# Two elementwise passes of a graph network: moving one operand of each VectorE operation from SBUF to PSUM

## The chip, the cores and the metric

The kernel runs on one core of a Trainium2 chip. The metric is the device time of one execution in microseconds (us). Engine names are those of the profile: PE (TensorE), DVE (VectorE), ACT (ScalarE), POOL (GpSimd), SP (SyncE, which here only issues transfers).

## The reference

Two graph layers on 6250 nodes of 512 features and 100000 edges, each with a layer norm and a ReLU ahead of it and a residual behind it. The change lies in the end of the second layer:

```python
score = exp(clip(einsum('ehd,ehd->eh', K[src], Q[dst]) * scale, -5, 5))   # 8 heads of 64
wV = segment_sum(V[src] * score, dst)
Z  = segment_sum(score, dst)
h  = h1 + wV / (Z + 1e-6)          # h1: the layer's input after norm and ReLU
mean, var = h.mean(0), h.var(0)    # over the 6250 nodes
out = x1 + (h - mean) * rsqrt(var + 1e-5) * gamma + beta
```

The last line is computed as `out = A*h + (x1 + C)`, with A and C one row of 512 numbers each, which stand repeated on all 128 partitions.

## The kernel before

The nodes lie in 49 windows of 128 (the last has 106). `sums` is a tile of SBUF that holds, for each window, 512 columns of wV and 8 columns of Z. Stages run one after the other, each a block that all engines leave together: preparation and layer 0, `dense` (norm, transposes and the three products of layer 1), `attend` (the gather over edges, which fills `sums`), and the three that matter here.

**First pass, `attended`.** DVE adds 1e-6 to all Z at once (L1280), takes their reciprocals in place (L1282), and then does two operations for each window: `weight` (L1288), which multiplies the window by its inverse counts, and `add_h1` (L1293), which adds the window of h1, both in place in `sums`. DVE's order is written out: weight of window w+1, then add_h1 of window w. SP loads h1 from HBM into four buffers in turn (L1234, 256 KB each); the load of window w waits for add_h1 of window w-4 (semaphore `made`, which starts at 4). Behind add_h1, three engines form the sums over the nodes: PE adds up the columns of the window with a matmul against ones (L926), ACT squares the window into one of four buffers `sq` (L1267), and POOL adds that square to `S2` (L1248, two inputs in SBUF) and waits for its own result before the next. None of these three holds DVE back, but the block ends only when all are done.

**Coefficients.** A and C are made from the sums in a chain of short operations (L967 to L1007).

**Last pass, `finish`.** SP loads x1 into four buffers in turn (L1317); the load of window w waits for the result of window w-4 (`done`, which starts at 4). POOL adds C to x1 in place (`shift`, L1341, two inputs in SBUF). DVE does two operations for each window: `scale` (L1353, window times A, in place) and `add` (L1360, window plus x1 into one of four buffers `o`). Its order is scale of window w+1, then add of window w. The add of window w waits for POOL's shift, for the scale, and for the store of window w-4, which has used the same `o`. ACT issues the stores (L1328) as soon as an add is done.

Of the kernel before, what the change touches and what calls it, by code (L numbers as in the profile page):

```python
# [24 lines left out]
ds = bass.ds  # L25
# [6 lines left out]
def build(nc, x, src, dst, W_l, b_l, W_r, gamma0, beta0, Wq, Wk, Wv, gamma1, beta1, out):  # L32
# [44 lines left out]
    with life:  # L77
# [1141 lines left out]
        def attended(S1, S2):  # L1219
            with ExitStack() as ctx:  # L1220
                h1 = sb(ctx, "h1b", [P, NB, D])
                sq = sb(ctx, "sq1", [P, NB, D])
                ps_1 = pb(ctx, "ps_1", [P, 512])
                zero2, h_in, inverse, weighted, made, squared, summed1, summed2 = (
                    sem("zeroed_S2"), sems("h_in2", NB), sem("inverse"), sem("weighted"), sem("h_made2"), sem("squared1"),
                    sem("summed1b"), sem("summed2b"))

                @nc_block()
                def _(block):
                    @block.sync  # L1230
                    def _(sp):
                        def load(w, b):
                            sp.wait_ge(made, w + 1)
                            sp.dma_start(h1[:, b, :], h1_d[ds(w * P, P), :]).then_inc(h_in[b], 16)  # L1234

                        with sp.Fori(0, FOURS) as i:
                            for b in range(NB):
                                load(NB * i + b, b)
                        load(WINDOWS - 1, 0)

                    @block.gpsimd
                    def _(pool):
                        nc.gpsimd.memset(S2[:, :], 0.0).then_inc(zero2, 1)
                        pool.wait_ge(zero2, 1)

                        def add_square(w, b, n=P):
                            pool.wait_ge(squared, w + 1)
                            nc.gpsimd.tensor_tensor(S2[0:n, :], S2[0:n, :], sq[0:n, b, :], ALU.add).then_inc(summed2, 1)  # L1248
                            pool.wait_ge(summed2, w + 1)

                        with pool.Fori(0, FOURS) as i:
                            for b in range(NB):
                                add_square(NB * i + b, b)
                        add_square(WINDOWS - 1, 0, LAST)

                    @block.tensor
                    def _(pe):
                        column_sums(pe, ps_1, made, NB, summed1)

                    @block.scalar  # L1260
                    def _(act):
                        def square(w, b):
                            act.wait_ge(made, w + NB + 1)
                            if not isinstance(w, int) or w >= NB:
                                act.wait_ge(summed2, w - NB + 1)
                            alone(act)
                            nc.scalar.activation(sq[:, b, :], window(w), ACT.Square).then_inc(squared, 1)  # L1267

                        for w in range(NB):
                            square(w, w)  # L1270
                        with act.Fori(1, FOURS) as i:
                            for b in range(NB):
                                square(NB * i + b, b)
                        square(WINDOWS - 1, 0)

                    @block.vector
                    def _(dve):
                        dve.sem_inc(made, NB)
                        weights = sums[:, :].rearrange("p (w c) -> p w c", c=WIDTH)[:, :, D:WIDTH]
                        nc.vector.tensor_scalar(weights, weights, 1e-6, None, ALU.add).then_inc(inverse, 1)  # L1280
                        dve.wait_ge(inverse, 1)
                        nc.vector.reciprocal(weights, weights).then_inc(inverse, 1)  # L1282
                        dve.wait_ge(inverse, 2)

                        def weight(w):
                            v = window(w).rearrange("p (h d) -> p h d", h=HEADS)
                            z = sums[:, ds(w * WIDTH + D, HEADS)].unsqueeze(2).to_broadcast([P, HEADS, DH])
                            nc.vector.tensor_tensor(v, v, z, ALU.mult).then_inc(weighted, 1)  # L1288

                        def add_h1(w, i, b):  # L1290
                            dve.wait_ge(h_in[b], 16 * (i + 1))
                            dve.wait_ge(weighted, w + 1)
                            nc.vector.tensor_tensor(window(w), window(w), h1[:, b, :], ALU.add).then_inc(made, 1)  # L1293

                        weight(0)
                        with dve.Fori(0, FOURS) as i:
                            for b in range(NB):
                                weight(NB * i + b + 1)
                                add_h1(NB * i + b, i, b)
                        add_h1(WINDOWS - 1, FOURS, 0)  # L1300
                        dve.wait_ge(summed1, WINDOWS)
                        share_of(S1, ps_1)


        def finish(A_bc, C_bc):
            with ExitStack() as ctx:
                x1 = sb(ctx, "x1b", [P, NB, D])
                o = sb(ctx, "o", [P, NB, D])
                x_in, shifted, scaled, done, stored = sems("x_in3", NB), sem("shifted"), sem("scaled1"), sem("done"), sems("stored_", NB)

                @nc_block()
                def _(block):
                    @block.sync
                    def _(sp):
                        def load(w, b):
                            sp.wait_ge(done, w + 1)
                            sp.dma_start(x1[:, b, :], x1_d[ds(w * P, P), :]).then_inc(x_in[b], 16)  # L1317

                        with sp.Fori(0, FOURS) as i:
                            for b in range(NB):  # L1320
                                load(NB * i + b, b)
                        load(WINDOWS - 1, 0)

                    @block.scalar
                    def _(act):
                        def store(w, b, n=P):
                            act.wait_ge(done, w + NB + 1)
                            act.dma_start(out[ds(w * P, n), :], o[0:n, b, :]).then_inc(stored[b], 16)  # L1328

                        with act.Fori(0, FOURS) as i:  # L1330
                            for b in range(NB):
                                store(NB * i + b, b)
                        store(WINDOWS - 1, 0, LAST)
                        for b in range(NB):
                            act.wait_ge(stored[b], 16 * (FOURS + (b == 0)))

                    @block.gpsimd
                    def _(pool):
                        def shift(w, i, b):
                            pool.wait_ge(x_in[b], 16 * (i + 1))  # L1340
                            nc.gpsimd.tensor_tensor(x1[:, b, :], x1[:, b, :], C_bc[:, :], ALU.add).then_inc(shifted, 1)  # L1341

                        with pool.Fori(0, FOURS) as i:
                            for b in range(NB):
                                shift(NB * i + b, i, b)
                        shift(WINDOWS - 1, FOURS, 0)

                    @block.vector
                    def _(dve):
                        dve.sem_inc(done, NB)  # L1350

                        def scale(w):
                            nc.vector.tensor_tensor(window(w), window(w), A_bc[:, :], ALU.mult).then_inc(scaled, 1)  # L1353

                        def add(w, i, b):
                            dve.wait_ge(shifted, w + 1)
                            dve.wait_ge(scaled, w + 1)
                            if not isinstance(i, int) or i:
                                dve.wait_ge(stored[b], 16 * i)  # L1359
                            nc.vector.tensor_tensor(o[:, b, :], window(w), x1[:, b, :], ALU.add).then_inc(done, 1)  # L1360

                        scale(0)
                        for w in range(NB):
                            scale(w + 1)
                            add(w, 0, w)
                        with dve.Fori(1, FOURS) as i:  # L1366
                            for b in range(NB):
                                scale(NB * i + b + 1)
                                add(NB * i + b, i, b)
                        add(WINDOWS - 1, FOURS, 0)  # L1370

# [36 lines left out]
```

## Time and profile before

| | us |
|---|---|
| median of 3 runs (3610.95 to 3612.53) | 3612.53 |
| the profiled execution | 3613.78 |
| its span, from the first instruction to the last | 3611.8 |
| first pass: DVE's first operation of the block to POOL's last | 3365.0 to 3480.3 |
| coefficients | 3480.8 to 3490.8 |
| last pass: first scale to last add | 3491.4 to 3604.6 |

Times of instructions are counted from the span's start. An engine's busy time is the time in which one of its instructions is under way, whether it moves data or is held up after its start; so a long instruction of a known size is the thing to look at, not the busy share. Two instructions of DVE overlap a little: the next starts before the one ahead of it has ended.

### The profile page before, as it was taken

How to read it: one execution, taken by the hardware profiler on the slowest of the kernel's cores; microseconds unless marked ns; L12 is line 12 of the kernel's file. 1: busy time of each engine (PE TensorE's matmuls, PEld its weight loads, DVE VectorE, ACT ScalarE, POOL GpSimd, SP SyncE). 2: the span in 40 equal slices, each digit the busy share in tenths (PEclk: the TensorE clock that was granted, in tenths of full speed). 3: DMA queues.
4: the chain of work that ended last, by engine and by line, in shares of the span. 5: the costliest groups of instructions: out<-in, count | busy, mean ns of one | idle time of the engine just before them, and what ended most of it. 6: DMA issues, size and time to landing. Idle time of an engine off the chain costs nothing. (4 is left out here: it accounts for less than half of the span.)

```text
span 3611.8 us, 59603 instructions
## 1 busy us (share of the span) xinstructions
PE 2939.7 (81%) x11648; PEld 1500.4 (42%) x11649; DVE 2479.0 (69%) x4591; ACT 1625.9 (45%) x6212; POOL 1891.1 (52%) x1929
## 2 busy tenths in 40 slices
PE   4977767777677774999989999999999999999640
PEld 2432222222222222888864444444444444444210
DVE  4643333333333334555559999999999999999999
ACT  2530000000000001222239999999999999999410
POOL 1017777777777771111135555555555555555456
PEclk9997787777777776999999999999999999999865
DMA  2447777777777772444459898888989889888347
GB/s 87 146 144 207 207 208 207 208 207 206 208 207 208 208 207 90 151 152 148 145 213 314 310 313 310 311 309 311 311 308 311 307 311 311 312 308 313 97 123 214
DMA packets 263475, 828.03 MB, mean 229 GB/s; under 512 B 35237, under 2 KB 35239, under 8 KB 263402
## 3 DMA queue, kind: packets, MB, share of 16 engines
q0 software_dynamic: 197504, 693.22, 59.4%
q1 hardware_dynamic: 58910, 121.60, 10.4%
q10 hardware_dynamic: 7020, 12.80, 0.9%
q14 instruction: 32, 0.26, 0.0%
q8 instruction: 9, 0.15, 0.0%
HBM read 750.45 MB, written 77.83 MB: 229 GB/s over the span
## 5 line engine op out<-in xcount | busy, mean ns | idle before, releaser
L1064 POOL DMA_INDIRECT kv<-kv_d,src_t x880 | 828.2, 941 | 677.4 <-PE psw L1204 510.4
L822 POOL DMA_INDIRECT rows<-y_d,src_t x880 | 844.1, 959 | 486.7 <-issue 244.6
L1085 ACT ACTIVATE kv<-kv,wgt 128x64 f32<-128x64 f32 x4400 | 1096.9, 334 | 0.0
L1201 PE MATMUL psa<-kv,hot 128*128 128x512 f32 x1760 | 863.4, 613 | 29.2 <-ACT kv L1085 28.0
L909 PE MATMUL pss<-rows,hot 128*128 128x512 f16 x1760 | 556.9, 447 | 276.0 <-DMA rows<-y_d,src_t 252.5
L1110 DVE TENSOR_TENSOR kv<-kv,ps_q 128x1024 f32<-128x1024 f32 x440 | 534.6, 1215 | 35.8 <-PE ps_q L1185 20.7
L1123 DVE TENSOR_REDUCE score<-kv 128x16 f32<-128x1024 f32 x440 | 533.5, 1212 | 0.0
L1007 ACT ACTIVATE var<-var 128x512 f32<-128x512 f32 x2 | 1.3, 629 | 1134.9 <-DVE var L994 1134.9
L1201 PEld LDWEIGHTS psa<-kv,hot 128*128 128x128 f32 x1760 | 303.6, 189 | 396.1 <-issue 386.9
L1185 PE MATMUL ps_q<-sums,hotT 128*128 x1760 | 454.9, 381 | 0.0
L843 DVE TENSOR_SCALAR rd<-psc 128x1 f32 (+1 forms) x49 | 7.8, 159 | 547.0 <-PE psc L911 547.0
L909 PEld LDWEIGHTS pss<-rows,hot 128*128 128x128 f16 x1760 | 120.0, 104 | 470.5 <-issue 411.4
L1204 PE MATMUL psw<-parts,hot 128*128 128x16 f32 x880 | 302.0, 415 | 0.0
L836 DVE TENSOR_TENSOR hot<-lane,rel_t 128x256 f16<-128x256 f32 x440 | 187.3, 426 | 163.3 <-issue 98.4
L344 POOL TENSOR_TENSOR x_sb<-x_sb,C_bc 128x512 f32<-128x512 f32 x49 | 63.5, 1297 | 410.7 <-DMA x_sb<-in_x 410.7
L1204 PEld LDWEIGHTS psw<-parts,hot 128*128 128x128 f32 x880 | 167.5, 190 | 211.0 <-issue 211.0
L1116 DVE TENSOR_TENSOR kv<-kv,wgt 128x384 f32<-128x384 f32 x440 | 242.6, 551 | 0.3 <-ACT wgt L1078 0.3
L510 PE MATMUL ps_o<-w_hi,hT_hi 128*128 128x512 f32 x588 | 239.5, 407 | 0.0
L510 PE MATMUL ps_o<-w_hi,hT_lo 128*128 128x512 f32 x588 | 232.2, 395 | 0.0
L510 PE MATMUL ps_o<-w_lo,hT_hi 128*128 128x512 f32 x588 | 231.7, 394 | 0.0
L1185 PEld LDWEIGHTS ps_q<-sums,hotT 128*128 128x128 f16 x1760 | 172.8, 98 | 110.6 <-issue 2.6
L893 PE MATMUL psz<-w_r,sums 128*128 128x512 f16 x588 | 214.7, 541 | 0.0
(185 smaller groups left out, 3550.8 us busy)
## 6 DMA issues: line engine op xcount, KB each, us to landing
kv_d<-o_sb SPq DMA_DIRECT2D x49, 512.0 KB, 2.9
rows<-y_d,src_t POOLq DMA_INDIRECT x880, 3.7
kv<-kv_d,src_t POOLq DMA_INDIRECT x880, 5.3
y_d<-y SPq DMA_DIRECT2D x49, 256.0 KB, 2.0
x_d<-x_sb SPq DMA_DIRECT2D x49, 256.0 KB, 3.2
h_d<-h SPq DMA_DIRECT2D x49, 256.0 KB, 3.4
h1b<-h_d SPq DMA_DIRECT2D x49, 256.0 KB, 2.7
x1b<-x_d SPq DMA_DIRECT2D x49, 256.0 KB, 4.0
```

The costliest lines, as they stand in the source:

```text
L510: last = nc.tensor.matmul(ps_o[par][k][:, :], a, b[:, k, c, :], start=(c == 0 and j == 0), stop=(c == KC - 1 and j == 2))
L822: pool.indirect_dma_start(rows[:, u, g, :], None, y_d[0:N, :], bass.IndirectOffsetOnAxis(src_t[:, m:m + 1], 0)).then_inc(rows_in[u], 16)
L893: nc.tensor.matmul(psz[:, ds(par, D)], slots[:, ds(at * 2 + part * D + c * P, P)], w_r16[:, of, c, :], start=(c == 0 and part == of == 0), ...
L909: nc.tensor.matmul(pss[:, ds(par, D)], hot[:, u, g, :], rows[:, u, g, part * D:(part + 1) * D], start=False, stop=(g == G - 1 and part == ...
L1064: pool.indirect_dma_start(kv[:, u, g, :], None, kv_d[0:N, :], bass.IndirectOffsetOnAxis(src_t[:, m:m + 1], 0)).then_inc(rows_in[u], 16)
L1085: last = nc.scalar.mul(v, v, wgt[:, u, g * HEADS + h:g * HEADS + h + 1])
L1110: nc.vector.tensor_tensor(k, k, ps_q[u % 2][:, :].rearrange("p (g d) -> p g d", g=G), ALU.mult).then_inc(multiplied, 1)
L1116: nc.vector.tensor_tensor(v, v, w.unsqueeze(3).to_broadcast([P, G, HEADS - HA, DH]), ALU.mult)
L1123: nc.vector.tensor_reduce(score[:, u, :].rearrange("p (g h) -> p g h", g=G), kv[:, u, :, 0:D].rearrange("p g (h d) -> p g h d", h=HEADS), ...
L1185: last = nc.tensor.matmul(ps_q[u % 2][:, g * D:(g + 1) * D], hotT[:, u % 2, g * P:(g + 1) * P], slots[:, ds(col * 2 + k * D, D)], start=(k ...
L1201: nc.tensor.matmul(pss[:, ds(par, D)], hot[:, u, g, :].bitcast(F32), kv[:, u, g, D:2 * D], start=False, stop=(g == G - 1), skip_group_chec ...
L1204: last = nc.tensor.matmul(psc[:, 0:2 * HEADS], hot[:, u, g, :], parts[:, u % 4, g, :, :].rearrange("p t h -> p (t h)"), start=False, stop= ...
```

## The change

The two passes keep their operations, their number and their order. Each operation of DVE now takes one of its two inputs from PSUM:

- the reciprocals are written to a tile `z_inv` in PSUM instead of back into `sums`;
- `weight` reads the window from SBUF and the inverse counts from PSUM, and writes to one of four tiles `ps_v` in PSUM;
- `add_h1` reads `ps_v` and h1 (SBUF), and writes the window in `sums`;
- A is copied once to `A_ps` in PSUM;
- `scale` reads the window from SBUF and A from PSUM, and writes to one of four tiles `ps_a` in PSUM;
- `add` reads `ps_a` and x1 (SBUF), and writes `o`.

As the four PSUM tiles are used in turn, `weight` and `scale` get a wait on the result of four windows earlier.

```diff
@@ attended
+                z = pb(ctx, "z_inv", [P, WINDOWS * HEADS])
+                ps_v = [pb(ctx, f"ps_v{k}", [P, D]) for k in range(NB)]
-                        nc.vector.reciprocal(weights, weights).then_inc(inverse, 1)
+                        nc.vector.reciprocal(z[:, :].rearrange("p (w h) -> p w h", h=HEADS), weights).then_inc(inverse, 1)
-                        def weight(w):
+                        def weight(w, b):
+                            dve.wait_ge(made, w + 1)
                             v = window(w).rearrange("p (h d) -> p h d", h=HEADS)
-                            z = sums[:, ds(w * WIDTH + D, HEADS)].unsqueeze(2).to_broadcast([P, HEADS, DH])
-                            nc.vector.tensor_tensor(v, v, z, ALU.mult).then_inc(weighted, 1)
+                            nc.vector.tensor_tensor(ps_v[b][:, :].rearrange("p (h d) -> p h d", h=HEADS), v,
+                                                    z[:, ds(w * HEADS, HEADS)].unsqueeze(2).to_broadcast([P, HEADS, DH]),
+                                                    ALU.mult).then_inc(weighted, 1)
@@ add_h1
-                            nc.vector.tensor_tensor(window(w), window(w), h1[:, b, :], ALU.add).then_inc(made, 1)
+                            nc.vector.tensor_tensor(window(w), ps_v[b][:, :], h1[:, b, :], ALU.add).then_inc(made, 1)
@@ finish
+                A_ps = pb(ctx, "A_ps", [P, D])
+                ps_a = [pb(ctx, f"ps_a{k}", [P, D]) for k in range(NB)]
+                A_in = sem("A_in")
+                        nc.vector.tensor_copy(A_ps[:, :], A_bc[:, :]).then_inc(A_in, 1)
+                        dve.wait_ge(A_in, 1)
-                        def scale(w):
-                            nc.vector.tensor_tensor(window(w), window(w), A_bc[:, :], ALU.mult).then_inc(scaled, 1)
+                        def scale(w, b):
+                            dve.wait_ge(done, w + 1)
+                            nc.vector.tensor_tensor(ps_a[b][:, :], window(w), A_ps[:, :], ALU.mult).then_inc(scaled, 1)
@@ add
-                            nc.vector.tensor_tensor(o[:, b, :], window(w), x1[:, b, :], ALU.add).then_inc(done, 1)
+                            nc.vector.tensor_tensor(o[:, b, :], ps_a[b][:, :], x1[:, b, :], ALU.add).then_inc(done, 1)
```

The calls of `weight` and `scale` get the number of the buffer, `(b + 1) % NB`, as their second argument.

## Rows read from the trace of the kernel before

**Rows 1.** The page: busy tenths of DVE, and GB/s, in 40 equal slices.
```profile
DVE  4643333333333334555559999999999999999999
...
GB/s 87 146 144 207 207 208 207 208 207 206 208 207 208 208 207 90 151 152 148 145 213 314 310 313 310 311 309 311 311 308 311 307 311 311 312 308 313 97 123 214
```

**Rows 2.** Busy time of each engine in the two passes, granted clock, DMA share, GB/s.
```profile
3371.00:3479.00 108.00, 72.27 (x98) 20.27 (x96) 106.71 (x94) 30.25 (x48) 68.90 (x48) 0.75 0.39 109
3495.00:3603.00 108.00, 0.00 (x0) 0.00 (x0) 106.46 (x95) 0.00 (x0) 73.11 (x49) 0.50 0.78 225
```

**Rows 3.** Instruction groups, 3280 to 3612 us: busy us, mean ns | idle before.
```profile
L1353 DVE TENSOR_TENSOR sums<-sums,A_bc 128x512 f32 (+1 forms) x49 | 62.0, 1267 | 0.6 <-PEq L102 0.6
...
L1293 DVE TENSOR_TENSOR sums<-sums,h1b 128x512 f32 (+1 forms) x49 | 58.8, 1202 | 0.0
L1288 DVE TENSOR_TENSOR sums<-sums (+1 forms) x49 | 57.9, 1183 | 0.0
L1360 DVE TENSOR_TENSOR o<-sums,x1b 128x512 f32<-128x512 f32 x49 | 54.5, 1114 | 3.8 <-POOL x1b L1341 3.8
```

**Rows 4.** Timeline of the first pass, two windows: start us, duration us, engine, line.
```profile
3421.22 1.35 POOL L1248 TENSOR_TENSOR S<-S,sq 128x512 f32<-128x512 f32 x1 [1.53 <-ACT sq L1267]
3421.37 1.75 DVE L1288 TENSOR_TENSOR sums<-sums  x1
...
3422.73 1.51 POOL L1248 TENSOR_TENSOR S<-S,sq 128x512 f32<-128x512 f32 x1 [0.16 <-POOL S L1248]
3423.05 1.75 DVE L1293 TENSOR_TENSOR sums<-sums,h1b 128x512 f32 x1
3424.72 0.68 DVE L1288 TENSOR_TENSOR sums<-sums  x1
```

**Rows 5.** Timeline of POOL in the first pass: its first and last operation.
```profile
3371.04 1.50 POOL L1248 TENSOR_TENSOR S<-S,sq 128x512 f32<-128x512 f32 x1 [5.62 <-ACT sq L1267]
...
3479.06 1.26 POOL L1248 TENSOR_TENSOR S<-S,sq 106x512 f32<-106x512 f32 x1 [0.23 <-POOL S L1248]
```

**Rows 6.** Timeline of the last pass: its start and its end.
```profile
3491.42 1.29 DVE L1353 TENSOR_TENSOR sums<-sums,A_bc 128x512 f32<-128x512 f32 x2 [0.62 <-PEq L102]
...
3495.39 0.69 DVE L1360 TENSOR_TENSOR o<-sums,x1b 128x512 f32<-128x512 f32 x1 [2.68 <-POOL x1b L1341]
...
3602.28 2.35 DVE L1360 TENSOR_TENSOR o<-sums,x1b 128x512 f32<-128x512 f32 x2
```

**Rows 7.** Timeline of the dense stage: two places where POOL and DVE meet.
```profile
1416.84 1.42 POOL L344 TENSOR_TENSOR x_sb<-x_sb,C_bc 128x512 f32<-128x512 f32 x1 [21.26 <-DMA x_sb<-in_x]
1417.16 1.64 DVE L384 TENSOR_TENSOR x_sb<-x_sb 128x512 f32<-128x512 f32 x1
...
1832.73 1.29 POOL L344 TENSOR_TENSOR x_sb<-x_sb,C_bc 128x512 f32<-128x512 f32 x1 [11.85 <-DMA x_sb<-in_x]
...
1833.17 0.69 DVE L355 TENSOR_TENSOR hT_lo<-ps_t,hT_hi 128x512 fp32r<-128x512 f32 x1
```

**Rows 8.** Line L407, a copy from PSUM in the dense stage: ns min/median/max.
```profile
L407 DVE COPY o_sb<-ps_o x49: 691/692/693, 1431.1 to 1854.7; 128x512 f32<-128x512 f32 x49
```

**Rows 9.** Tile x1b, POOL's shift in the last pass: ns min/median/max.
```profile
L1341 POOL TENSOR_TENSOR x1b<-x1b,C_bc x49: 1256/1521/1813, 3494.1 to 3602.1; 128x512 f32<-128x512 f32 x49
```

**Rows 10.** Timeline of PE in the first pass: two windows are four matmuls.
```profile
3411.29 3.57 PE L926 MATMUL ps<-sums,ones 128*128 x4 [1.28 <-DVE sums L1293]
3415.84 2.33 PE L926 MATMUL ps<-sums,ones 128*128 x4 [0.97 <-DVE sums L1293]
```

**Rows 11.** DMA issues of the two passes: KB each, median us to landing.
```profile
h1b<-h_d SPq DMA_DIRECT2D x44, 256.0 KB, 2.7
...
result<-o ACTq DMA_DIRECT2D x47, 256.0 KB, 4.2
x1b<-x_d SPq DMA_DIRECT2D x45, 256.0 KB, 4.0
```

**Rows 12.** Waits of SP's queue in the last pass: us in total, times, longest.
```profile
SPq L1317 <- DVE o L1360: 75.2, 45, 2.9
```

More of the change, by code:

```diff
@@ L1292, in add_h1 @@
                             dve.wait_ge(weighted, w + 1)
-                            nc.vector.tensor_tensor(window(w), window(w), h1[:, b, :], ALU.add).then_inc(made, 1)
-                        weight(0)
+                            nc.vector.tensor_tensor(window(w), ps_v[b][:, :], h1[:, b, :], ALU.add).then_inc(made, 1)
+                        weight(0, 0)
                         with dve.Fori(0, FOURS) as i:
                             for b in range(NB):
-                                weight(NB * i + b + 1)
+                                weight(NB * i + b + 1, (b + 1) % NB)
                                 add_h1(NB * i + b, i, b)
@@ L1359, in add @@
                                 dve.wait_ge(stored[b], 16 * i)
-                            nc.vector.tensor_tensor(o[:, b, :], window(w), x1[:, b, :], ALU.add).then_inc(done, 1)
-                        scale(0)
+                            nc.vector.tensor_tensor(o[:, b, :], ps_a[b][:, :], x1[:, b, :], ALU.add).then_inc(done, 1)
+                        scale(0, 0)
                         for w in range(NB):
-                            scale(w + 1)
+                            scale(w + 1, (w + 1) % NB)
                             add(w, 0, w)
@@ L1367, in _ @@
                             for b in range(NB):
-                                scale(NB * i + b + 1)
+                                scale(NB * i + b + 1, (b + 1) % NB)
                                 add(NB * i + b, i, b)
```

## The prediction

> **What bounds the kernel now.** I read the page's slices first, to see which stretch the change can touch. DVE is busy nine tenths or more from the middle of the kernel to its end, and the rate of the transfers drops sharply in the slices ahead of the last [rows 1]: the two changed passes are the last three slices or so, about 225 us of 3612. What comes before them is not edited and I leave it alone.
>
> Next the two passes by themselves, as stretches [rows 2]: DVE is busy for 106.7 of 108 us in the one and 106.5 of 108 in the other. That looks like DVE as the bound, so the next view is what its instructions take, by line [rows 3]. All four kinds are 128 x 512 fp32, one element per lane and step, yet their means lie between 1114 and 1267 ns. A mean over equal shapes that is that uneven in four lines asks for the single instructions, and the timeline gives them [rows 4]: an operation takes either 0.68 or 1.75 us. The reader is to look at what POOL does beside each long one. POOL begins a tensor_tensor with two SBUF inputs at 3421.22; DVE's operation begins at 3421.37 and takes 1.75. The next POOL operation begins at 3422.73, DVE's at 3423.05, and that takes 1.75 again; then comes one of 0.68 with no POOL operation just begun. Successive DVE operations overlap by 0.08 (3423.05 + 1.75 = 3424.80, and the next starts at 3424.72), so a free one costs 0.60 and a held one 1.67. The difference, 1.07 us, is the hold. One window has two DVE operations and one POOL operation: 2 x 0.60 + 1.07 = 2.27 us. Over 48 windows that is 109 us, which is what both passes take: the first from POOL's start at 3371.04 to 3480.32 [rows 5], the last from the first add at 3495.39 to that of the last window, 0.68 before the merged row's end at 3604.63 [rows 6]. So DVE is "busy", but for 1.07 of each 2.27 us it stands behind POOL.
>
> Does PSUM free it? The dense stage shows both cases [rows 7]. At 1417.16 a DVE addition with both inputs in SBUF (L384) begins 0.32 us into a POOL addition and takes 1.64. At 1833.17 one with an input in PSUM and one in SBUF (L355) begins 0.44 us into a POOL addition, ends before it, and takes 0.69. A copy out of PSUM (L407), which in that stage usually meets POOL's addition, never takes more than 693 ns in 49 [rows 8]. So POOL holds DVE where both of DVE's inputs are in SBUF, and not where one is in PSUM. That is the case of all four changed operations.
>
> **The first pass, part by part.** Nothing is removed but the holds: 48 x 1.07 = 51 us of DVE. DVE would then need 2 x 0.60 = 1.20 us a window. What is late next? POOL. Its own operation without DVE in the way is the last one of the pass, 1.26 us, on 106 partitions but as many columns [rows 5]; the shortest of 49 in the last pass, on 128, is 1.256 [rows 9]. Between two of them it waits 0.16 us for its own result [rows 4], so 1.42 us a window. From the same start, 3371.04, it ends at 48 x 1.42 + 1.26 = 69.4 us later, 3440.5, where it now ends at 3480.3. **Gain 39.9 us.** ACT's squares need 30.25 / 48 = 0.63 a window [rows 2] and follow. PE's two matmuls need 2.33 / 2 = 1.17 where they are short [rows 10], below 1.42. h1 lands 2.7 us after its issue [rows 11]; with the add behind it, 0.7, and some 0.3 of handing over, a buffer's lap is 3.7 us, and DVE comes back to a buffer after 4 x 1.20 = 4.8. This cover goes only if the landing grows above 3.8; until POOL itself starved it would have to reach 4.7.
>
> The reciprocal into PSUM stays one instruction. The new wait of weight (window w behind add_h1 of w-4) is met 4.8 us before it is asked; behind it stands only the following add_h1. I price both at nothing; if the wait were ever open, DVE has 0.22 us a window to give before POOL notices.
>
> **The last pass.** The copy of A and its wait come ahead of the first scale: about 0.7 us, one operation of this size, plus a handover. Now DVE does two scales from 3491.42 to 3492.71 and then idles 2.68 us for the first shift [rows 6], which covers the copy; without cover it would cost 0.8. The scale's new wait is met three adds earlier. From the first add on, the holds go (1.07 a window), and again something else is late. POOL's shift allows 1.26. The ring of buffers allows less: an add lets SP load the next window into the buffer, 4.0 us to land [rows 11], 1.26 for the shift, 0.68 for the add, and some 0.3 for three handovers: 6.2 us for a lap of four windows, 1.56 a window. Now the lap is 4 x 2.27 = 9.1, so it has slack, and SP's queue stands waiting for DVE's add, 45 times and 1.67 us each [rows 12]; these loads and the stores (4.2 us to land, no shift behind them, so a lap of 5.2) will start sooner. What they collide with is each other: load and store of one window are released by the same add, 512 KB in all, and the DMA engines are already taken for 0.78 of the time at 225 GB/s [rows 2]. At full share and the same time per packet that is 288 GB/s, or 524288 B / 288 = 1.82 us a window. The fastest long stretches of the page reach 307 to 314 GB/s [rows 1], which would be 1.67. I take 1.70 (308 GB/s), as the stretch of the page is sustained and the 288 is scaled from packets that also queue; the ends are 1.56 (lap at today's landing) and 1.82. **Gain 48 x (2.27 - 1.70) = 27.4 us**, between 21.6 and 34.1.
>
> A page rates such transfers higher: the Trainium skill, "SBUF — State Buffer", section "Summary: rules for kernel authors", has about 358 GB/s for transfers between HBM and SBUF. By it 512 KB would be 1.46 us, an estimate from that page, and the transfers would not be the bound; no run here shows that rate with 2 KB rows going both ways.
>
> **Sum.** 3613.78 - 39.9 - 27.4 = 3546.5 by the profiled execution, which lies 1.25 above the median of the runs. The median would be 3545; I add 0.8 for the copy, should its cover fail: **3546 us**, 1.8% faster.
>
> **Rivals.**
> *PE ends the first pass.* The same two windows take PE 3.57 us instead of 2.33 in places [rows 10], and the granted clock of the pass is 0.75 of full [rows 2], so it changes between its two levels, 2.4 and 1.2 GHz. At 3.57 / 2 = 1.79 a window throughout, the pass would last 49 x 1.79 = 88 us, a gain of 21 instead of 40: 3564. Against it: PE idles 1 to 2 us between its groups now, and will be fed a window each 1.2 us, hence have work always.
> *The transfers are no bound in the last pass.* If landings fall toward the 2.7 us that loads without stores show [rows 11], the lap is 4.9 / 4 = 1.23 and POOL's 1.26 decides: up to 48 x (1.70 - 1.26) = 21 us more, 3525 to 3540. Against: the share of 0.78.
> *Operations that write PSUM are dear.* No DVE operation of the trace writes PSUM. Reading it costs 0.69 against 0.68. If a write doubled the 0.60 of weight and scale, DVE would need 1.80 a window in both passes: 2 x 48 x 0.47 = 45 us of gain, 3568. The Trainium skill ("Perfetto Trace Analysis", "Optimizing Scalar/DVE Operations") puts a DVE access to PSUM at about 125 ns against 60 for SBUF; an estimate by that page is a pair of 1.33 us, which would use up most of DVE's margin to POOL but not the gain. The reads of the trace show 10 to 15 ns.
> *The hold stays.* If POOL held DVE for one SBUF input too, or if DVE held by its PSUM output, both passes keep 2.27: 3613, no change. Against it stands L355.
> *Slower.* The same price of a PSUM write decides. weight or scale would have to cost more than 0.60 + 1.07 = 1.67 us, 2.8 times the read, for the pair to pass 2.27; at three times, 1.80 + 0.60 = 2.40 a window, 2 x 48 x 0.13 = 12 us lost, 3625. Nothing in the rows points there.
>
> **Numbers.** Chances: forecast 0.66 (its own range 3537 to 3554); PE 0.08; no transfer bound 0.10; dear writes 0.08; hold stays 0.04; slower 0.04. The range from 3534 to 3564 takes in the forecast, PE and half of the faster case, 0.79. Faster by more than 0.2% (7 us, about what a measurement of this kernel can tell from no change): 0.92; same 0.04; slower 0.04.
>
> **What would show it.** First pass: no DVE operation above 0.75 us; POOL's squares at 1.26 each and back to back at 1.42, DVE done some 10 us before POOL, a pass of about 70 us. If PE decides, L938 waits for PE long after POOL's end. Last pass: DVE idle before the adds, waiting for POOL's shift, and POOL waiting for x1; a DMA share near 0.95 at about 308 GB/s; landings of 4.3 to 5 us. Long DVE operations that begin inside a POOL operation would refute the release; uniform ones above 0.75 us would mean a dear PSUM access.

## The result, and the profile after

The changed kernel takes 3547.3 us (median of 4 runs, 3544.1 to 3547.9) against 3612.5: a ratio of 0.982, 95% interval 0.980 to 0.984. The forecast was 3546. The profiled execution took 3547.64 us; its span is 3545.7.

Where the 66.1 us between the two profiled executions lie, from the start and end times of the two traces:

| stretch | before | after | difference |
|---|---|---|---|
| up to POOL's first square (edited only in its last 6 us) | 3371.0 | 3369.3 | -1.8 |
| POOL's first square to the end of its last | 109.3 | 72.5 | -36.8 |
| on to DVE's first operation of the last pass | 11.1 | 12.4 | +1.3 |
| on to the first add | 4.0 | 5.1 | +1.1 |
| first add to the end of the last add | 109.2 | 79.5 | -29.7 |
| the last store | 7.2 | 7.0 | -0.2 |

The groups by line of the changed kernel, 3280 to 3546 us (busy us, mean ns of one, idle time of the engine before them and what ended it), answer to [rows 3]:

```profile
L1250 POOL TENSOR_TENSOR S<-S,sq 128x512 f32<-128x512 f32 (+1 forms) x49 | 62.2, 1270 | 15.9 <-POOL S L1250 10.1 <-ACT sq L1269 5.8
L1348 POOL TENSOR_TENSOR x1b<-x1b,C_bc 128x512 f32<-128x512 f32 x49 | 61.6, 1263 | 34.7 <-DMA x1b<-x_d 34.1
...
L1371 DVE TENSOR_TENSOR o<-ps_a,x1b 128x512 f32<-128x512 f32 x49 | 33.9, 691 | 21.1 <-POOL x1b L1348 20.8
L1364 DVE TENSOR_TENSOR ps_a<-sums,A_ps 128x512 f32<-128x512 f32 x49 | 33.5, 686 | 0.0
L1290 DVE TENSOR_TENSOR ps_v<-sums,z_inv 128x512 f32 (+1 forms) x49 | 33.4, 684 | 0.0
L1297 DVE TENSOR_TENSOR sums<-ps_v,h1b 128x512 f32 (+1 forms) x49 | 33.0, 676 | 0.0
```

Every DVE operation is back at 0.67 to 0.70 us: the means have fallen from between 1114 and 1267 ns and are now even, which is the sign that nothing holds them. The two traces bear this out operation by operation. Before, 96 of the 196 DVE operations of the two passes begin while a POOL addition is under way, and 94 of these take 1.73 us or more; of the other 100 none takes more than 0.70. After, 124 begin while a POOL addition is under way, and none takes more than 0.70. POOL's operations gain as well, 1.27 against 1.43 to 1.52, since DVE no longer stands in their way either. The idle time has changed hands: DVE, which had almost none, now waits 20.8 us for POOL's shift.

The two passes as stretches, the first and then the last, answer to [rows 2]:

```profile
3371.00:3441.00 70.00, 52.56 (x96) 14.29 (x94) 54.94 (x92) 29.60 (x47) 59.90 (x48) 0.91 0.56 165
...
3460.00:3538.00 78.00, 0.00 (x0) 0.00 (x0) 60.02 (x94) 0.00 (x0) 59.46 (x48) 0.50 0.93 309
```

The timeline of the first pass (PE's, then POOL's and DVE's rows) answers to [rows 4, 5, 10]:

```profile
3368.51 58.27 PE L926 MATMUL ps<-sums,ones 128*128 128x512 f32 x98 [6.44 <-DVE sums L1297]
...
3369.29 1.27 POOL L1250 TENSOR_TENSOR S<-S,sq 128x512 f32<-128x512 f32 x1 [5.62 <-ACT sq L1269]
...
3373.58 1.27 POOL L1250 TENSOR_TENSOR S<-S,sq 128x512 f32<-128x512 f32 x1 [0.16 <-POOL S L1250]
3373.75 0.68 DVE L1297 TENSOR_TENSOR sums<-ps_v,h1b 128x512 f32 x1
3374.35 0.69 DVE L1290 TENSOR_TENSOR ps_v<-sums,z_inv 128x512 f32 x1
...
3375.26 1.27 POOL L1250 TENSOR_TENSOR S<-S,sq 128x512 f32<-128x512 f32 x1 [0.41 <-POOL S L1250]
...
3440.54 1.26 POOL L1250 TENSOR_TENSOR S<-S,sq 106x512 f32<-106x512 f32 x1 [0.23 <-POOL S L1250]
```

DVE's operations at 3373.75 and 3374.35 lie wholly or in large part inside POOL's of 3373.58 to 3374.85 and take 0.68 and 0.69. POOL now sets the pass: (3440.54 - 3369.29) / 48 = 1.484 us a window. PE follows DVE, which gives it a window every 1.18 us (its adds start at 3367.8 to 3424.6): 98 matmuls in 58.27 us, 1.19 a window, done 15 us before POOL.

The last pass in the timeline, its copy, first add and last add, answers to [rows 6]:

```profile
3454.16 0.69 DVE L1359 COPY A_ps<-A_bc 128x512 f32<-128x512 f32 x1 [0.62 <-PEq L102]
...
3459.23 0.69 DVE L1371 TENSOR_TENSOR o<-ps_a,x1b 128x512 f32<-128x512 f32 x1 [3.04 <-POOL x1b L1348]
...
3538.06 0.69 DVE L1371 TENSOR_TENSOR o<-ps_a,x1b 128x512 f32<-128x512 f32 x1 [0.82 <-POOL x1b L1348]
```

(3538.06 - 3459.23) / 48 = 1.642 us a window. The waits of that pass (3460 to 3538 us: total, times, longest), SP's queue last, and its DMA issues:

```profile
POOL x1b L1348 <- DMA x1b<-x_d: 17.9, 29, 1.1
DVE o L1371 <- POOL x1b L1348: 16.9, 29, 1.0
...
SPq L1324 <- DVE o L1371: 44.4, 44, 1.7
```

```profile
result<-o ACTq DMA_DIRECT2D x48, 256.0 KB, 4.7
x1b<-x_d SPq DMA_DIRECT2D x45, 256.0 KB, 4.4
```

The three waits close a ring: POOL waits for x1, DVE waits for POOL, and SP waits for DVE's add before it may load again.

### The profile page after: what moved, and what is told of

Same layout as the page of the kernel before. It is cut to its first block and busy times, and to the rows that moved or that the text cites. A ratio compares the mean times of both kernels' runs of the same rounds, so it can differ in the third digit from the quotient of the medians.

```text
span 3545.7 us, 59651 instructions
## 1 busy us (share of the span) xinstructions
PE 2925.5 (83%) x11648; PEld 1495.4 (42%) x11649; DVE 2381.9 (67%) x4592; ACT 1625.2 (46%) x6212; POOL 1870.1 (53%) x1929
## 5 line engine op out<-in xcount | busy, mean ns | idle before, releaser
L909 PE MATMUL pss<-rows,hot 128*128 128x512 f16 x1760 | 564.0, 452 | 270.8 <-DMA rows<-y_d,src_t 248.2
```

The source lines that it names most:

```text
L909: nc.tensor.matmul(pss[:, ds(par, D)], hot[:, u, g, :], rows[:, u, g, part * D:(part + 1) * D], start=False, stop=(g == G - 1 and part == ...
```

## The experiments

Two theories stood against each other on why DVE is freed: POOL holds DVE's operations that have both inputs in SBUF (the memory decides), or the operations gain because they no longer work in place and have buffers between them (the dependences decide). A third question is what bounds each pass now. All kernels were compared with the kernel before on the same chip, at 3611.8 to 3612.3 us. The changed kernel was not run again beside them, so a difference from it compares separate groups of runs; the times that are compared spread by some 5 us within a group.

### One pass at a time

The functions of the other pass are those of the kernel before.

```diff
 e1: attended as in the changed kernel      | e2: attended as before
 e1: finish as before                       | e2: finish as in the changed kernel
```

> Only the first pass takes operands from PSUM; the last pass is that of the kernel before. If POOL's port hold is the cause and the two passes are independent, the first pass goes from 109 us (POOL's first to last square) to 72.5 as in the changed kernel and the last pass keeps 2.26 us a window: 3612.5 - 37 = 3575, plus up to 1 us for slower matmuls in the coefficients, which follow a longer idle time of PE. If the gain in one pass were given back in the other, it would be nearer 3612 or nearer 3547.

Measured: 3575.9 us, ratio 0.990 (0.989 to 0.992). POOL's squares run from 3367.2 to 3438.5, 1.485 us a window; the last pass stays at 2.26.

> Only the last pass takes operands from PSUM. Port hold and independent passes: the last pass goes to 1.64 us a window, 30 us less between the first and the last add, 1 us lost ahead of them to the copy of A: 3612.5 - 29 = 3584. Rival, gains that depend on each other: 3612 or 3547.

Measured: 3582.8 us, ratio 0.992 (0.990 to 0.994). The adds of the last pass run at 1.62 us a window; the first pass stays at 2.25. The two gains, 35.9 and 29.0, add up to 64.9; both together gave 65.2. The passes are independent.

### The same program with its tiles in SBUF

```diff
-                z = pb(ctx, "z_inv", [P, WINDOWS * HEADS])
-                ps_v = [pb(ctx, f"ps_v{k}", [P, D]) for k in range(NB)]
+                z = sb(ctx, "z_inv", [P, WINDOWS * HEADS])
+                ps_v = [sb(ctx, f"ps_v{k}", [P, D]) for k in range(NB)]
...
-                A_ps = pb(ctx, "A_ps", [P, D])
-                ps_a = [pb(ctx, f"ps_a{k}", [P, D]) for k in range(NB)]
+                A_ps = sb(ctx, "A_ps", [P, D])
+                ps_a = [sb(ctx, f"ps_a{k}", [P, D]) for k in range(NB)]
```

> The changed kernel with its new tiles (z_inv, ps_v, ps_a, A_ps) in SBUF: same operations, same buffers, same waits, only the memory differs. Port hold theory: all holds are back, 2.26 us a window in both passes, 3613. Rival, that operations gain because they no longer work in place or because the buffers uncouple them: 3547.

Measured: 3614.3 us, ratio 1.0007 (0.9997 to 1.0016). Its groups by line:

```profile
L1297 DVE TENSOR_TENSOR sums<-ps_v,h1b 128x512 f32 (+1 forms) x49 | 58.8, 1202 | 0.0
L1364 DVE TENSOR_TENSOR ps_a<-sums,A_ps 128x512 f32<-128x512 f32 x49 | 58.8, 1201 | 0.0
L1371 DVE TENSOR_TENSOR o<-ps_a,x1b 128x512 f32<-128x512 f32 x49 | 58.7, 1200 | 3.4 <-POOL x1b L1348 3.4
```

The means are back at 1200 ns with the same buffers and the same waits. The whole gain hangs on the memory, none of it on working out of place.

### Only the adds read PSUM

```diff
-                z = pb(ctx, "z_inv", [P, WINDOWS * HEADS])
+                z = sb(ctx, "z_inv", [P, WINDOWS * HEADS])
...
-                A_ps = pb(ctx, "A_ps", [P, D])
+                A_ps = sb(ctx, "A_ps", [P, D])
```

> The inverse counts and A stay in SBUF, so weight and scale have two SBUF inputs (they still write PSUM); the adds read PSUM. Port hold theory: a POOL operation holds the port 1.07 us and runs beside the add (0.60) for free; only what is left, about 0.47 us, delays weight or scale, so 1.67 us a window at least in both passes, 1.67 to 1.85: first pass 82 to 90 us, total 3555 to 3575. Rival, that each POOL operation costs DVE 1.07 us wherever it falls: 2.27, 3613. Rival, that writing out of place is what counts: 3547.

Measured: 3560.9 us, ratio 0.986 (0.985 to 0.988). POOL's squares run from 3368.1 to 3449.4, 1.69 us a window, and the adds of the last pass from 3466.5 to 3549.3, 1.73. The timeline of the first pass:

```profile
3402.08 1.27 POOL L1250 TENSOR_TENSOR S<-S,sq 128x512 f32<-128x512 f32 x1 [0.45 <-ACT sq L1269]
3402.10 0.68 DVE L1297 TENSOR_TENSOR sums<-ps_v,h1b 128x512 f32 x1
3402.70 1.21 DVE L1290 TENSOR_TENSOR ps_v<-sums,z_inv 128x512 f32 x1
```

Add and POOL's operation begin together, and the add takes 0.68 beside it. Then weight, with two SBUF inputs, finds POOL still at work and is held 0.53 us; by the median of all 49 weights, 1.17 us, the hold is 0.49, and 0.47 was expected. So it is not the POOL operation that costs DVE 1.07 us but only the part of it that meets an operation with two SBUF inputs. A PSUM output did not free weight here; a PSUM input does in the changed kernel.

### What bounds the passes now: two accumulators, and eight buffers

In e5, POOL adds even and odd windows into two tiles, so that an operation needs the one before last and not the last (S2b is zeroed at the start, and the first four windows stand ahead of the loop):

```diff
-                            nc.gpsimd.tensor_tensor(S2[0:n, :], S2[0:n, :], sq[0:n, b, :], ALU.add).then_inc(summed2, 1)
-                            pool.wait_ge(summed2, w + 1)
+                            acc = (S2, S2b)[b % 2]
+                            if not isinstance(w, int) or w >= 2:
+                                pool.wait_ge(summed2, w - 1)
+                            nc.gpsimd.tensor_tensor(acc[0:n, :], acc[0:n, :], sq[0:n, b, :], ALU.add).then_inc(summed2, 1)
...
+                        pool.wait_ge(summed2, WINDOWS)
+                        nc.gpsimd.tensor_tensor(S2[:, :], S2[:, :], S2b[:, :], ALU.add).then_inc(zero2, 1)
```

> The changed kernel, and in its first pass POOL adds the squares of even and odd windows into two tiles, so that it no longer waits for the operation just ahead; one more POOL operation at the end joins them. If POOL ends the first pass, its pace goes from 1.48 us a window to 1.25 to 1.30, and the pass from 72.5 to some 62 plus 1.4 us: 9 us less, 3538. Rival, that PE or DVE ends the pass at nearly POOL's pace now: 0 to 3 us less.

Measured: 3540.1 us, ratio 0.980 (0.978 to 0.982), 7 us less than the changed kernel (9 between the two profiled executions). POOL in the timeline, two windows, and the joining operation:

```profile
3426.37 1.31 POOL L1255 TENSOR_TENSOR S2b<-S2b,sq 128x512 f32<-128x512 f32 x1
3427.60 1.30 POOL L1255 TENSOR_TENSOR S<-S,sq 128x512 f32<-128x512 f32 x1
...
3431.42 1.26 POOL L1264 TENSOR_TENSOR S<-S,S2b 128x512 f32<-128x512 f32 x1
```

1.23 us a window, with no gap. From the first square to the end of the joining operation the pass takes 61.7 us in place of 72.5. POOL's wait for itself was what the first pass had left.

In e6, the last pass has eight buffers each for x1 and for the results (R in place of NB in `finish`, four PSUM tiles as before):

```diff
-                x1 = sb(ctx, "x1b", [P, NB, D])
-                o = sb(ctx, "o", [P, NB, D])
+                x1 = sb(ctx, "x1b", [P, R, D])
+                o = sb(ctx, "o", [P, R, D])
...
-                            dve.wait_ge(done, w + 1)
+                            dve.wait_ge(done, w + R - NB + 1)
```

> The changed kernel with eight buffers instead of four for x1 and for the results of the last pass. If the transfers bound the last pass (share 0.93 at 309 GB/s), the pace stays between 1.58 and 1.64 us a window and landings grow to some 9 or 10 us: 0 to 4 us less, 3545. Rival, the lap of the four buffers bounds it (4.4 us to land + 2.2 = 6.6, 1.64 a window): with eight the lap allows 0.9 to 1.3, POOL's 1.27 decides, 17 us less, 3530.

Measured: 3527.9 us, ratio 0.977 (0.975 to 0.978), 19 us less than the changed kernel. POOL's shifts as one merged row of the timeline, and the stretch from 3460 to 3515 us:

```profile
3457.80 60.47 POOL L1350 TENSOR_TENSOR x1b<-x1b,C_bc 128x512 f32<-128x512 f32 x49 [16.23 <-DMA x1b<-x_d]
```

```profile
3460.00:3515.00 55.00, 0.00 (x0) 0.00 (x0) 54.87 (x90) 0.00 (x0) 54.88 (x46) 0.50 1.05 400
```

49 shifts without a break in 60.47 us, 1.23 a window, at 400 GB/s. The first alternative of the expectation is refuted: the transfers did not bound the changed kernel at 309; the lap of the four buffers did.

The DMA queues show what became of a packet's time (loads, then stores: packets, MB, share of the 16 engines): the kernel before from 3495 to 3603 us, the changed kernel from 3460 to 3538, e6 from 3460 to 3515.

```profile
q1 hardware_dynamic: 6695, 12.17, 48.8%
q10 hardware_dynamic: 6664, 12.14, 29.2%
...
q1 hardware_dynamic: 6480, 11.80, 52.4%
q10 hardware_dynamic: 6768, 12.32, 41.1%
...
q1 hardware_dynamic: 6249, 11.37, 54.4%
q10 hardware_dynamic: 5810, 10.59, 50.0%
```

A load's packet took 126 ns before (48.8% of 16 x 108 us, over 6695 packets), 101 ns in the changed kernel and 77 ns in e6; a store's packet took 76 ns in all three.

In e8 only x1 has eight buffers, the results keep four:

```diff
-                o = sb(ctx, "o", [P, R, D])
+                o = sb(ctx, "o", [P, NB, D])
```

(against e6, with the stores and their waits counted to match)

> The changed kernel with eight buffers for x1 but four for the results, in the last pass. If it is the lap of the x1 buffers alone that bounds the changed last pass, this is as fast as eight of both, 3528, 1.23 us a window. If the results' buffers are close behind (4.7 us for a store to land, 0.7 for the add, 0.3 of handing over: 5.7, 1.43 a window, more if the stores land later at the higher pace), 1.43 to 1.6 a window, 3537 to 3545.

Measured: 3537.5 us, ratio 0.980 (0.978 to 0.981). The adds run from 3459.7 to 3527.7, 1.42 a window, and a new wait has come up, on the stores:

```profile
DVE o L1373 <- DMA result<-o: 7.5, 18, 1.5
```

So the second ring lies where its own lap puts it: a store lands in 4.8 us here, 4.8 + 1.0 = 5.8, over four 1.45.

In e9 the kernel before gets the eight buffers of e6:

```diff
-                x1 = sb(ctx, "x1b", [P, NB, D])
-                o = sb(ctx, "o", [P, NB, D])
+                x1 = sb(ctx, "x1b", [P, R, D])
+                o = sb(ctx, "o", [P, R, D])
```

> The kernel before with eight buffers for x1 and for the results. If POOL's hold alone set its last pass, 2 x 0.60 + 1.07 = 2.27 us a window stay whatever the buffers allow: 3612. Rival, that the four buffers had a part in it: up to 40 us less.

Measured: 3612.3 us, ratio 1.0001 (0.9991 to 1.0011), the adds from 3493.9 to 3602.3, 2.26 a window. Before the change the buffers cost nothing; the same edit is worth 19 us after it.

### The two remedies together

e7 is the changed kernel with the edits of e5 and e6.

> Both of the former. If the passes are independent, the sum of their gains: 3536 where the transfers bound the last pass, 3520 where the lap does.

Measured: 3518.2 us, ratio 0.974 (0.973 to 0.976), the fastest kernel of the study: 29 us less than the changed one, of which e5 gave 7 and e6 19. The sum would be 26; the 3 us beyond it are within the spread of e5's runs (3536.6 to 3541.4), and its two passes are as fast here as in e5 and e6 within 0.5 us (61.7 and 60.4 us).

## Why the prediction was right, step by step

**The hold.** Right, and shown: 0.68 and 1.75 us before, 0.67 to 0.70 after, all of it back when the tiles lie in SBUF (e3), nearly half of each hold, 0.49 of 1.07 us at the median, back when one operation of the pair has two SBUF inputs (e4). The rivals "the hold stays", "dear writes" and "slower" fall: the operations that write PSUM take 0.684 and 0.686 us on average. For the effect of the other memory on DVE, the Trainium skill ("Perfetto Trace Analysis", "Optimizing Scalar/DVE Operations") gives about 125 ns on PSUM against 60 on SBUF, 65 more; the rows show 15 ns or less (medians of 674 to 691 ns with a PSUM input, 676 to 679 for operations with SBUF alone that are not held), and the measurement decides. On the hold itself, the Trainium skill ("SBUF — State Buffer", "Who interferes with whom") says that a DVE instruction with two SBUF inputs contends with a GpSimd one that reads SBUF. The runs agree: 1.75 us beside POOL with two SBUF inputs, 0.68 with one in PSUM.

**First pass: POOL at 1.42 us a window, gain 39.9.** Right in the mechanism, 3.1 us too much in size. The term that was off is the wait between two squares: I took 0.16 for all, but at every fourth, where the loop turns, it is 0.41 (the row at 3375.26). 48 x (1.484 - 1.42) = 3.1. Before the change POOL waited 40.7 us for ACT's squares and 4.0 for itself, never more than 0.23 at a time; with two accumulators (e5) the gap is gone. The rival "PE ends the pass" did not come true: PE kept up with DVE at 1.19 us a window, at a granted clock of 1.00 (2.4 GHz) from 3371 to 3426, against 0.75 over the pass before.

**Last pass: transfers at 308 GB/s, 1.70 us a window, gain 27.4.** The number was close (1.642 and 29.7), and the rate and the DMA share fell where they were put (309 GB/s, 0.93), but the step behind them was wrong. "At full share and the same time per packet that is 288 GB/s" takes the share for a part of a capacity and a packet's time for fixed. Neither holds: with more buffers the same engines moved 400 GB/s at a share of 1.05, which can only come about where the times of packets overlap, and a load's packet took 126 ns before, 101 after and 77 in e6, so that part of its time was not moving. Why it falls as the pace rises stays open. What bound the pass was the lap that I had priced at 1.56 and set aside as the lower end: 4.4 us to land in place of 4.0, plus 1.26 for the shift, 0.69 for the add and 0.27 of handing over is 6.6, and a quarter of that is 1.65. The landing grew by 0.4 as the pace rose; that growth is the part that the transfers had in it, and that it comes from transfers crowding closer is likely but was not shown by itself. So the close number is luck: the rate of 308 GB/s was taken from another stretch of the profile's page and happened to lie near what the lap allows. The signs that I had set for it (share, rate, landings, both waits) came true as well, because a lap that is too short gives the same ones; only more buffers told the two apart. The rival "the transfers are no bound" was right about the transfers and wrong about the time, as it let the landing fall to 2.7. The Trainium skill's 358 GB/s ("SBUF — State Buffer", "Summary: rules for kernel authors"), by which I had noted that the transfers would not bind, pointed the right way, and the 400 GB/s of e6 go beyond it.

**The small edits.** The copy of A was taken to be hidden in DVE's wait for the first shift, and 0.8 us was added to the sum in case it was not. DVE still waits 3.04 us for that shift, so the cover holds; the stretch is 1.1 us longer because the first load took longer: from its issue to the first shift there are 3.6 us in place of 2.5. That is not the copy's doing: it was 2.7 in e2, which has a copy into PSUM, 2.9 in e1, which has none, and 3.7 in e3. What sets it stays open. Not foreseen were 1.3 us in the coefficients. PE has now stood idle 15.5 us when they begin, and their first two matmuls take 2.04 us in place of 1.10; the granted clock is 0.50 (1.2 GHz) from 3442.2 to 3446.2, where it was 1.00 (2.4 GHz) in the same place before. In e2, e3 and e9, whose first pass is as long as before, it is 11.1 us from POOL's last square to DVE's first operation of the last pass, as before.

**The sum.** That 3546 came within 1.3 us of 3547.3 is partly luck, as the errors cancel: 3.1 us too much gain in the first pass, 2.3 too little in the last, 2.4 lost between them where 0.8 was allowed, and 2.0 gained in stretches that the change hardly touches, whose length differs by a few us from one execution to the next (the first square begins at 3367.2 in e1 and at 3373.2 in e2).

## What to carry to other kernels

Where DVE looks full, compare the durations of single instructions of one shape: two values with POOL at work beside the longer one mean a hold, and one of two inputs in PSUM removes it, while a PSUM output alone does not. Price the next bound not by the DMA share but by the lap of the buffers, with landing times that grow with the pace; test it with more buffers, after the change and not before, as an edit that is worth nothing behind a hold can be worth 0.5% once the hold is gone. A self-wait of an engine and the turn of its loop count in full as soon as that engine sets the pace.

## What the hardware showed that was not expected

- The DMA share is no measure of what is left: 0.78 at 225 GB/s, 0.93 at 309, 1.05 at 400, all with the same transfers of 256 KB. The Trainium skill ("SBUF — State Buffer", "Summary: rules for kernel authors") has about 358 GB/s for transfers between HBM and SBUF; 55 us at 400 GB/s, loads and stores together, are above that, and the measurement decides for this kernel, which runs on one core; what a core gets while others move data no run here shows.
- At 400 GB/s landings were no longer steady: they rose along the pass of e6, from 3.6 us for the first load to 8.1 for the last, so even there the loads fell slowly behind POOL's 1.23 us a window. That pace asks for 425 GB/s (524288 B / 1.233 us); from the fifth of the 40 slices of that stretch on, the rate stood at 402 to 408. So the transfers were at a limit there; what sets it was not measured. The slices and the landings of e6:

```profile
GB/s 301 326 362 393 404 405 405 407 405 402 407 405 407 405 405 407 405 405 407 405 407 407 405 404 408 407 405 405 405 405 407 405 408 407 404 408 404 405 405 407
...
DMA to landing us min/median/max: 3.6/6.3/8.1
```

- POOL gains from the release too: its additions fell from 1.43 us (squares) and 1.52 us (shifts) on average to 1.27 and 1.26, and are back at 1.43 and 1.53 in e3.
